# The steps of attention spread anew between the products, and the loads of W1 put ahead of the x stores

## The reference

```
c   = x @ W + b + (x @ lora_A[m]) @ lora_B[m] * 2      # a LoRA adapter m for each sequence
q, k, v = c @ wq, c @ wk, c @ wv                       # 32 query heads, 8 key and value heads of 128
q, k = rope(q), rope(k)
o   = softmax(causal(q @ k.T * 128**-0.5)) @ v         # each sequence by itself, window 256 of 64 tokens
x   = x + o @ wo
x   = x + ffn(cond2(x))                                # two gated linear layers, folded ahead into one
```

## Time and profile before

| what | us |
|---|---|
| median of three runs | 3009.34 |
| the profiled execution | 3012.09 |
| its span | 3010.0 |
| TensorE busy (91% of the span) | 2733.9 |
| VectorE busy (45%) | 1352.2 |
| GpSimd busy (39%) | 1188.8 |
| ScalarE busy (29%) | 871.5 |
| stage of the fold | 0 to 154 |
| W1, half 0 / half 1 | 154 to 345 / 1592 to 1764 |
| attention, half 0 / half 1 | 345 to 989 / 1764 to 2405 |

### The profile page before, as it was taken

One profiled execution on the slowest core, in us unless ns is written; L12 is line 12 of the kernel. 1 busy time (PEld: TensorE's weight loads), 2 busy tenths in 40 slices (PEclk: granted clock), 3 DMA queues, 4 the chain that ended last, 5 costly groups with the idle time before them and its releaser, 6 DMA issues.

```text
span 3010.0 us, 37398 instructions
## 1 busy us (share of the span) xinstructions
PE 2733.9 (91%) x14520; PEld 2187.9 (73%) x14520; DVE 1352.2 (45%) x2011; ACT 871.5 (29%) x2089; POOL 1188.8 (39%) x790
## 2 busy tenths in 40 slices
PE   8967888988998899999998788888988889999999
PEld 7855767767777688887876567777776767888787
DVE  3121666666666311124533257676666621112452
ACT  2121333444433322211202124443444432221110
POOL 0023555555554444420303355555554444442030
PEclk9988999999999999999999899999999999999999
DMA  6843112222122453111452311212222334311142
GB/s 214 234 113 98 49 43 70 71 71 70 58 71 71 157 172 104 50 49 43 123 130 84 97 50 57 64 50 70 71 71 71 117 124 151 105 49 42 56 110 67
DMA packets 311472, 268.46 MB, mean 89 GB/s; under 512 B 67962, under 2 KB 283130, under 8 KB 311298
## 3 DMA queue, kind: packets, MB, share of 16 engines
q1 hardware_dynamic: 249698, 210.50, 23.1%
q10 hardware_dynamic: 61600, 55.58, 5.6%
HBM read 201.88 MB, written 64.16 MB: 88 GB/s over the span
## 4 chain that ended last, share of the span: by engine, by line
PE 68%; DMA 7%; issue 7%; DVE 7%; POOL 6%; ACT 3%; SPq 1%; ACTq 0%; DVEq 0%; POOLq 0%
PE prod L648 20%; PE prod L650 20%; PE prod L649 20%; DMA o_scratch<-o_out 6%; PE turned L837 2%; ACT o_out L1235 2%; POOL w_lo L1416 2%; POOL o_lo L1481 1%; DVE rope_sin L1663 1%; POOL x_sum L1434 1%; DVE neg_max L1689 1%; PE turned L642 1%; POOL s_lo L1451 1%; PE turned L870 1%; PE prod L1068 1%
## 5 line engine op out<-in xcount | busy, mean ns | idle before, releaser
L1416 POOL TENSOR_TENSOR w_lo<-raw,w_hi 128x1024 fp32r<-128x1024 f32 x96 | 233.5, 2433 | 925.2 <-ACT w_hi L1128 803.7
L648 PE MATMUL prod<-o_hi,w_hi 128*128 128x512 f32 x1024 | 403.8, 394 | 25.2 <-DVE rope_sin L1663 17.2
L649 PE MATMUL prod<-o_lo,w_hi 128*128 128x512 f32 x1024 | 400.6, 391 | 0.0
L650 PE MATMUL prod<-o_hi,w_lo 128*128 128x512 f32 x1024 | 400.3, 391 | 0.0
L1451 POOL TENSOR_TENSOR s_lo<-w_sum,s_hi 128x512 fp32r<-128x512 f32 x192 | 250.9, 1307 | 303.9 <-ACT s_hi L1196 303.9
L1765 DVE TENSOR_TENSOR x<-prod,x 128x512 f32<-128x512 f32 x128 | 88.5, 692 | 594.6 <-PE prod L650 594.6
L1128 ACT CAST w_hi<-raw 128x1024 fp32r<-128x1024 f32 x128 | 134.2, 1049 | 747.8 <-PE prod L650 429.2
L648 PE MATMUL prod<-t_hi,s_hi 128*128 128x512 f32 x768 | 314.6, 410 | 0.0
L650 PE MATMUL prod<-t_hi,s_lo 128*128 128x512 f32 x768 | 302.4, 394 | 0.0
L649 PE MATMUL prod<-t_lo,s_hi 128*128 128x512 f32 x768 | 301.8, 393 | 0.0
L648 PE MATMUL prod<-b_hi,s_hi 128*128 128x512 f32 x576 | 234.9, 408 | 15.8 <-POOL s_lo L1451 15.8
(11 more groups left out here) (168 smaller groups left out, 5103.7 us busy)
## 6 DMA issues: line engine op xcount, KB each, us to landing
raw_pair<-in_wq SPq DMA_DIRECT2D x64, 512.0 KB, 4.5
o_scratch<-o_out ACTq DMA_DIRECT2D x64, 512.0 KB, 2.9
raw<-in_wo SPq DMA_DIRECT2D x64, 512.0 KB, 3.9
o_raw<-o_scratch SPq DMA_DIRECT2D x64, 512.0 KB, 7.7
raw<-t_scratch SPq DMA_DIRECT2D x50, 512.0 KB, 4.7
t_scratch<-x ACTq DMA_DIRECT2D x17, 512.0 KB, 4.8
x_raw<-in_x SPq DMA_DIRECT2D x16, 512.0 KB, 5.2
xt_scratch<-x_sum SPq DMA_DIRECT2D x16, 512.0 KB, 3.4
```

Of the source, the lines that this page charges most:

```text
L648: pe.matmul(dst, wh, xh, start=start, stop=False)
L649: pe.matmul(dst, wh, xl, start=False, stop=False)
L650: return pe.matmul(dst, wl, xh, start=False, stop=stop)
L1416: pool.tensor_tensor(WL[i % 2][:], RAW[i % 2][:], WH[i % 2][:].bitcast(F32), ALU.subtract).then_inc(w_lo, 1)
```

## The change

It touches five places. (1) In attention, TensorE's list puts `turn_v` after 01.6, 23.0, 23.2 and 23.4 instead of 01.2 to 01.5, `pv` after KV.6, 01.1, 01.3 and 01.5 instead of KV.6, 01.0, 01.1 and 01.2, and the first `turn_p` after 23.6 instead of 23.5. ScalarE's list is rewritten so that each step stands behind the high part of the same number. VectorE's `mask` moves to the front of its pair, the second `mask` and the `normalise` ahead of U4, and the other `normalise` ahead of C21. (2) In W1 the load of tile n stands ahead of the store of x block n-3, and the second set of LoRA rows is loaded in two halves of the columns, after tiles 3 and 7. (3) x has eight buffers; in half 0 blocks 0 to 3 are loaded during the fold, 4 to 6 ahead of the LoRA loads. (4) The products use the PSUM banks in an order turned by two (`QB`), so that wo's first four products wait for one bank each. (5) In the first pair of a half GpSimd's two sums stand behind two low parts, and the places of two buffers change.

```diff
-        XR = [sb(f"x_raw{i}", [P, D], offset=4 * i * KB) for i in range(4)]
+        XR = [sb(f"x_raw{i}", [P, D], offset=o * KB) for i, o in enumerate((0, 4, 8, 12, 36, 40, 44, 32))]
...
+        QB = PJ[2:] + PJ[:2]
...
             for i in range(2, KC + 1):
+                if 4 <= i < 8:
+                    load_x(0, i - 4)
...
                     load_w1(0, 0)
                     load_w1(0, 1)
+                    for b in range(4, TB - 1):
+                        load_x(0, b)
                     sp.wait_ge(tw_turned, TW_N)
                     load_a1(0)
-                for b in range(4, TB):
-                    load_x(hf, b)
+                    load_x(0, TB - 1)
...
-                load_b1(hf, 0)
+                load_b1(hf, 0, slice(0, D))
                 for n in range(2, T_WO):
-                    if n - 2 < TB:
-                        store_xt(hf, n - 2)
                     load_w1(hf, n)
+                    if 0 <= n - 3 < TB:
+                        store_xt(hf, n - 3)
+                    if n == 6:
+                        sp.wait_ge(prod, q_base + QN["c3.0"] + 1)
+                        load_b1(hf, 1, slice(0, NT))
                     if n == 10:
                         sp.wait_ge(prod, q_base + QN["c7.0"] + 1)
-                        load_b1(hf, 1)
+                        load_b1(hf, 1, slice(NT, D))
...
                                 if at_ == (QD_01, 0):
-                                    pv(gg - 1, 0, 1)
                                     turn_p(gg - 1, 1, 1)
                                 if at_ == (QD_01, 1):
+                                    pv(gg - 1, 0, 1)
+                                if at_ == (QD_01, 3):
                                     pv(gg - 1, 1, 0)
-                                if at_ == (QD_01, 2):
+                                if at_ == (QD_01, 5):
                                     pv(gg - 1, 1, 1)
-                            if at_ == (QD_01, 2):
+                            if at_ == (QD_01, 6):
                                 turn_v(gg, 0)
-                            if at_ == (QD_01, 3):
+                            if at_ == (QD_23, 0):
                                 turn_v(gg, 1)
-                            if at_ == (QD_01, 4):
-                                turn_v(gg, 2)
-                            if at_ == (QD_01, 5):
-                                turn_v(gg, 3)
                             if at_ == (QD_23, 1):
                                 score(gg, 0, 0)
+                            if at_ == (QD_23, 2):
+                                turn_v(gg, 2)
                             if at_ == (QD_23, 3):
                                 score(gg, 0, 1)
-                            if at_ == (QD_23, 5):
+                            if at_ == (QD_23, 4):
+                                turn_v(gg, 3)
+                            if at_ == (QD_23, 6):
                                 turn_p(gg, 0, 0)
...
-                            if kb == 0 and j < 2:
-                                pe.wait_ge(rs_in, rotated_at(last_gg, QD_23, 3))
+                            if q == Q_WO:
+                                pe.wait_ge(quad_in, quad_at(pair_no(hf, NKV - 1, QD_23), A_U3))
+                            elif q < Q_WO + 4:
+                                pe.wait_ge(rs_in, rotated_at(last_gg, QD_23, q - Q_WO))
...
+                    if n == pair_no(hf, 0, 0):
+                        low(0, a11, 1)
+                        low(1, a12, 2)
                     pool.tensor_tensor(ta, a21, a22, ALU.add).then_inc(s_sum, 1)
```

More of the change, by code:

```diff
@@ L182, in build @@
         RAWP = sb("raw_pair", [P, 2 * D], offset=160 * KB)
-        SH = [sb(f"s_hi{i}", [P, NT], F32R, offset=(168 + 4 * i) * KB) for i in range(7)]
-        SL = [sb(f"s_lo{i}", [P, NT], F32R, offset=(170 + 4 * i) * KB) for i in range(7)]
+        s_at = (168, 176, 172, 180, 184, 188, 192)
+        SH = [sb(f"s_hi{i}", [P, NT], F32R, offset=s_at[i] * KB) for i in range(7)]
+        SL = [sb(f"s_lo{i}", [P, NT], F32R, offset=(s_at[i] + 2) * KB) for i in range(7)]
         AF32 = sb("small_out", [P, TOK], offset=112 * KB)
@@ L241, in build @@
         tw_stored = [sem(f"tw_stored{i}") for i in range(4)]
-        x_in = [sem(f"x_in{b}") for b in range(4)]
+        x_in = [sem(f"x_in{b}") for b in range(TB)]
         a_in = sem("a_in")
@@ L435, in load_tw, with load_x @@
                 sp.dma_start(dst, src).then_inc(tw_in[n % 4], 16)
+            def load_x(hf, b):
+                if hf == 0 and b >= 4:
+                    r = (b - 3) % 4
+                    sp.wait_ge(m_out[r], 16 * (KC // 4 + (r == 0)))
+                sp.dma_start(XR[b][:], x[hf * TOK + b * P:hf * TOK + (b + 1) * P, :]).then_inc(x_in[b], 16)
             for n in range(4):
@@ L621, in _ @@
                         if s in (2, 3):
-                            load_x(hf + 1, 2 * (s - 2))
-                            load_x(hf + 1, 2 * (s - 2) + 1)
+                            for b in range(4 * (s - 2), 4 * (s - 2) + 4):
+                                load_x(hf + 1, b)
                         if s == KC - 2:
@@ L801, in product @@
                     pe.wait_ge(s_lo, 7 * n + LOS[i])
-                    if i == 0 and first:
-                        pe.wait_ge(taken, q_base + Q_WO + 4)
+                    if i < 4 and first:
+                        pe.wait_ge(taken, q_base + Q_WO - 4 + i + 1 + 4)
                     elif i == 0:
@@ L1250, in _ @@
                         more = not (g == NKV - 1 and qd == QD_23)
-                        v0 = 4 * (gg - 1) if qd == QD_KV else 4 * gg
-                        p1_copy(n)
-                        if qd == QD_KV and g:
-                            p_out(4 * (gg - 1) + 1)
-                        if qd == QD_01 and g:
-                            p_out(4 * (gg - 1) + 3)
-                            o_out(gg - 1, 0, 1)
-                        if more:
-                            s_high(n + 1, 0)
-                            s_high(n + 1, 1)
@@ L1261, in _ @@
-                        if qd == QD_01 and g:
-                            o_out(gg - 1, 1, 0)
-                        if more:
-                            s_high(n + 1, 2)
-                        if qd == QD_KV and g:
-                            exps(4 * (gg - 1) + 2)
-                        if qd == QD_23:
-                            exps(4 * gg)
-                        if qd == QD_01:
-                            if g:
-                                o_out(gg - 1, 1, 1)
-                            v_out(gg, 0)
-                            v_out(gg, 1)
@@ L1750, in _ @@
                             normalise(4 * gg + 1)
+                        if not kv:
+                            add_head(A_C21, PR_4, XU[:], 1, 0, 2)
                         dve.wait_ge(quad_in, quad_at(n, A_U4))
```

106 lines of the change are left out of this document (60 added, 46 removed).

## The result

The changed kernel took 2831.22 us (median of four runs, 2826.46 to 2835.03), the kernel before 3009.32 beside it: a ratio of 0.9409, with a 95% interval of 0.9388 to 0.943. The forecast was 2829. The profiled execution is the fastest of the four, 2826.46, with a span of 2824.5, so 185.5 us less than the span of before, where the sum said 180.2.

A forecast was written before the change was run, and what follows sets the result against it. TensorE, busy 91% of the span, was taken as the bound, with some 276 us of waiting. Gains 106.6 + 78.4 - 2.0 + 0.9 - 3.7 = 180.2 off 3012.1 gave 2831.9, or 2829 as median; range 2790 to 2868.

The forecast's parts named there:

- 106.6 against 107.0: Attention: the forecast gain was 106.6 us, 83 from twelve steady groups and 23.6 from the first and last groups.
- the first groups: First group of each half: 8.4 us of waits go, 3.0 comes back from GpSimd's later sums, 5.4 gained each.
- the content of 71.9: Steady attention group: TensorE's time without waits, taken as the middle of 71.4 and 72.4 us.
- the 2.0 of waiting: Attention: the chain from product KV.4 to `pv` leaves 2.0 us of waiting at that `pv`, 14 times.
- the rival of VectorE late: Attention: VectorE's steps, held by GpSimd, end 1.09 us late, two a group in 14 groups; 31 more, 2860; chance 0.16.
- 76.4 against 75.5: W1, both halves: loads ahead of stores gain 78.4 us, less 1.0 a half for slower products.
- the pace of undisturbed tiles, 6.35: W1: a tile takes 6.35 us without waits, read from two late tiles where no load lies behind a store.
- the rival that they hold SyncE: W1: four half loads of LoRA rows cost 8.7 us each by holding SyncE's queue; 34.8, 2864; chance 0.12.
- 0.9 against 4.2: x transposes: the 10.6 us wait for `x_raw` goes, but `xt_lo` stands behind it; only 0.9 gained.
- -3.7 against -2.8: Start of wo: GpSimd's `o_lo` sets the start despite new banks; ScalarE's high part 1.9 us later each time, costing 3.7.
- The raw weights: Attention: ScalarE's steps wait behind the reload of `raw_pair`, 8.2 us in 48 pairs; 395 more, 3224; chance 0.02.
- waited for GpSimd's sum and not for a DMA: Attention, steady pairs: what ScalarE waited for in the kernel before, given as the argument against the raw-weights rival.

The follow-up runs named there:

- sum_early: The changed kernel with GpSimd's sum for block 3 in a buffer of its own, ahead of two low parts; span 2799.8 us.
- w1_only: The kernel before with one edit: in W1 the load of tile n stands ahead of the store of x block n-3; span 2944.6 us.
- banks_old: The changed kernel with the PSUM banks in the order of before; span 2828.4 us.
- norm_first: The changed kernel with VectorE's normalise of the first map of heads 2 and 3 ahead of the mask of the second; span 2850.6 us.
- rows_whole: The changed kernel with the second set of LoRA rows loaded at one time after tile 7, as before; span 2843.7 us.

## Why the prediction came out right, and where it did not

**Attention's size.** 106.6 against 107.0, but two misses of 9 us cancel. The sum gave 10.8 to the first groups, where the stretch to the first score gave 1.8; the other groups gave 105.2, where 95.8 were left for them. A steady group was near: the content of 71.9 is 71.5 in sum_early, the 2.0 of waiting is 1.78, and before and after differ by 7.3 in place of 6.9. No run put the old lists of attention back by themselves. That the 107 come from them is read from the waits, which lost 97.8, and from two runs beside it: with the old lists and the new queue a group stayed above 80 (w1_only), and with the new lists and the old banks it took 73.5 to 73.8 (banks_old).

**Its place.** The step "2.0 us of waiting turn up at that `pv`" failed by three quarters: 0.43 is there, and 1.35 at the transpose before it. That part is the rival of VectorE late. Its normalise took 1.73 where it began behind GpSimd's sum, and 0.69 in sum_early, where it began ahead of GpSimd's low part and that took longer instead. The Trainium skill, "SBUF — State Buffer", section "Who interferes with whom", says that a VectorE instruction with two inputs in SBUF must share a read port with GpSimd's reads; the normalise is one, and these rows agree with it. As a price the rival was wrong all the same: its 31 us would have come on top, while norm_first shows that without the lateness the wait stands at `pv`.

**What I left out.** By norm_first, a wait in one piece would have cost some 1.5 us more a group through the clock, 20 us in 13 of 14 groups, and the time would have been about 2849. The forecast took 2.0 in one piece and no such cost, so it was right in size partly by luck: the wait was split. Whether the split or the size spared the clock (1.78 in two pieces, 2.12 in one) no run separates.

**W1.** 76.4 against 75.5, and the cause is the one named: the store's wait for its sum. But only 51.4 of the 75.5 are waits; the other 24.1 are the same matmuls at a higher granted clock (0.84 and 0.82 before, 1.00 and 0.97 now), which the prediction names only as a small cost after the waits that stay. Its size came out because it set the whole stretch against the pace of undisturbed tiles, 6.35, and so took in both. The queue and the LoRA rows overlap, since 33 and 10.8 are more than the 38.8 of half 0. The half loads were hidden, and the rival that they hold SyncE is out: rows_whole shows 19 for splitting them. The rule weighed in the prediction, to join small transfers (the Trainium skill, "DMA: Bandwidth & Descriptors", "Rules for kernel authors"), would have them joined; here the measurement decides for the split, since nobody waits for the transfers' overhead: a half load of 32 KB takes 1.7 us from issue to landing, a whole one of 64 KB 2.0 in rows_whole.

**x.** 0.9 against 4.2, of which 1.9 arose before the first transpose of x, where runs differ by as much. The rest, 2.2, is more than the term, but it is not shown to be the edit: from the first transpose of x to tile 2 it was 49.8 before, 47.5 to 49.1 in the runs with eight buffers, and 48.7 in w1_only with four. The wait moved to `xt_lo` as forecast (7.8 in place of 10.6). The eight buffers were not tried by themselves.

**wo.** -3.7 against -2.8, and both halves of the reasoning hold: the banks give nothing, and ScalarE's later high part costs.

**The raw weights.** The prediction named a wait of ScalarE for `raw_pair` inside attention as a sign of being wrong, and the sign is there. The view of that tile has what ScalarE's high parts stood idle for in the changed kernel (us, times):

```profile
  DMA raw_pair<-in_wq: 90.4, 32
  DMA raw_pair<-in_wv: 41.3, 14
```

That is 131.7 us in 46 waits, and there are 48 pairs. The kernel before has 51.2 in 32, so "waited for GpSimd's sum and not for a DMA" was true of the pair in the earlier trace rows and not of most. In the steady groups these waits cost TensorE nothing that its list shows. It pays in one place, the first group of a half, where it waits 5.7 for a copy of v. On ScalarE:

```profile
352.75 0.62 ACT L1213 CAST s_hi<-w_sum 128x512 fp32r<-128x512 f32 x1 [7.44 <-POOL w_sum L1489]
...
354.31 0.57 ACT L1244 COPY v_tok<-turned 128x512 f32<-128x512 f32 x1
```

The copy stands behind a high part that waited 7.44 for GpSimd's sum, in a pair whose first high part had waited 6.42 for the reload. TensorE waited there before the change too, up to 6.7, and the sum was wrong to count that wait among those that go: this is the larger part of the first groups' miss.

## What to carry to other kernels

Work out what a stretch takes with no wait, then ask which chain is too long to fit; the first gives the floor (71.5 here) and the second what stays. When a wait has moved, look for the operation that stands in both chains, as one GpSimd sum did here, rather than for the operation named by the wait. Look at the order within one queue as well as within an engine: putting a load ahead of a store that waits was worth 28 us a half by itself (w1_only), twice what moving GpSimd's sum gave (13 to 14 a half), though less than all of attention's new lists together (about 53).

## What the runs showed of the hardware

After a wait of 2.12 us at `pv` the granted clock was 0.57 over the next 4.0 us in one group shown, and 13 of 14 groups were slower by 1.5 us; the fourteenth waited the same 2.12 and kept 1.00. After 1.35 and 0.43 with a product between it was 1.00. A wait's length alone does not decide it: ahead of tile 2 TensorE waited 3.81 in the changed kernel and went on at full pace, while in norm_first, after the same 3.81, the first matmuls took 0.63 in place of 0.39.

In the rows shown, where a VectorE and a GpSimd instruction overlapped, the one that began second took longer: VectorE's normalise 1.73 in place of 0.69 where it began 0.09 behind GpSimd's sum, and GpSimd's low part 1.84 in place of 1.29 where it began 0.01 behind the normalise.
